# Second layer: where the hidden value of some routed and final items is kept, and which engine splits it

## The reference, cut to what matters

```
# second layer, L1
for e in range(2):                                  # shared experts
    h = silu(x @ s_w1[e].T) * (x @ s_w3[e].T);  shared += h @ s_w2[e].T
for e in range(8):                                  # routed experts, all computed, gates mostly zero
    h = gelu(x @ r_w1[e].T);                    routed += h @ r_w2[e].T * gates[:, e]
y = (shared / 2 + routed) / 4
out = x + (gelu((y @ U1) @ V1 + b1) @ U2) @ V2 + b2   # low-rank final block, 512 hidden features
```

## Time and profile before

| what | value |
|---|---|
| time, median of 3 runs | 890.18 us (889.91 to 892.35) |
| span of the profiled execution, first to last instruction | 886.9 us |
| what lies around the span, against the median | 3.3 us |
| TensorE busy | 870.3 us, 98% |
| VectorE busy | 682.8 us, 77% |
| ScalarE busy | 574.0 us, 65% |
| GpSimd busy | 402.0 us, 45% |
| granted TensorE clock | 1.000 of full |

### The profile page before, as it was taken

One profiled execution on the slowest core, in us unless ns is written; L12 is line 12 of the kernel. 1 busy time (PEld: TensorE's weight loads), 2 busy tenths in 40 slices (PEclk: granted clock), 3 DMA queues, 4 the chain that ended last, 5 costly groups with the idle time before them and its releaser, 6 DMA issues.

```text
span 886.9 us, 12606 instructions
## 1 busy us (share of the span) xinstructions
PE 870.3 (98%) x3838; PEld 690.2 (78%) x3838; DVE 682.8 (77%) x1094; ACT 574.0 (65%) x1029; POOL 402.0 (45%) x376
## 2 busy tenths in 40 slices
PE   8999999999999999999999999999999999999997
PEld 5788888777888888888888888888888777777773
DVE  7877777869689786686686686686665888998887
ACT  7888888765555455555555555555555678989895
POOL 7557783135356453253253252252232227754462
PEclk9999999999999999999999999999999999999999
DMA  9589981023113112012012012011010049582700
GB/s 311 211 276 313 293 295 35 1 86 135 48 48 111 42 42 84 4 45 84 1 48 83 1 48 84 0 48 48 1 48 0 1 108 209 106 178 53 161 25 36
DMA packets 36404, 83.23 MB, mean 94 GB/s; under 512 B 4464, under 2 KB 14320, under 8 KB 34544
## 3 DMA queue, kind: packets, MB, share of 16 engines
q1 hardware_dynamic: 36336, 82.42, 30.1%
HBM read 71.39 MB, written 6.83 MB: 88 GB/s over the span
## 4 chain that ended last, share of the span: by engine, by line
PE 76%; DVE 9%; issue 4%; ACT 3%; SPq 3%; DMA 2%; POOL 1%; DVEq 0%; ACTq 0%; POOLq 0%
PE ps L932 16%; PE ps L951 16%; PE ps L937 16%; PE ps L992 8%; PE ps L994 8%; PE ps L987 8%; DVE HL L1571 3%; SPq L658 1%; PE ps L974 1%; PE ps L972 1%; DVE Hf L1551 1%; DMA ST<-scratch 1%; DVE Hf L1558 1%; ACT HH L1084 1%; SPq L771 1%
## 5 line engine op out<-in xcount | busy, mean ns | idle before, releaser
L1078 ACT ACTIVATE Sg<-ps 128x512 f32<-128x512 f32 x288 | 171.7, 597 | 242.6 <-PE ps L951 242.3
L1551 DVE TENSOR_TENSOR Hf<-ps,Sg 128x512 f32<-128x512 f32 x288 | 197.9, 688 | 147.7 <-ACT Sg L1078 97.5
L1663 POOL TENSOR_TENSOR HL<-Hf,HH 128x512 fp32r<-128x512 f32 x130 | 174.2, 1347 | 157.4 <-ACT HH L1084 141.0
L1084 ACT ACTIVATE HH<-Hf 128x512 fp32r<-128x512 f32 x346 | 216.1, 625 | 21.1 <-DVE Hf L1551 14.4
L1571 DVE TENSOR_TENSOR HL<-Hf,HH 128x512 fp32r<-128x512 f32 x248 | 220.1, 888 | 4.3 <-ACT HH L1084 3.2
L932 PE MATMUL ps<-XHL,WBH 128*128 128x512 f32 x512 | 203.7, 398 | 1.8 <-DVE Hf L1551 1.8
L951 PE MATMUL ps<-XHL,WBH 128*128 128x512 f32 x512 | 202.2, 395 | 0.0
L937 PE MATMUL ps<-XHL,WBL 128*128 128x512 f32 x512 | 202.0, 395 | 0.0
L1678 POOL TENSOR_TENSOR XT<-XT,TMP 128x512 f32<-128x512 f32 x64 | 84.0, 1312 | 248.9 <-DVE TMP L1425 248.7
L932 PEld LDWEIGHTS ps<-XHL,WBH 128*128 128x128 f32 x512 | 96.0, 188 | 27.0 <-DVE Hf L1551 4.0
L951 PEld LDWEIGHTS ps<-XHL,WBH 128*128 128x128 f32 x512 | 96.0, 188 | 23.0
(11 more groups left out here) (275 smaller groups left out, 1327.6 us busy)
## 6 DMA issues: line engine op xcount, KB each, us to landing
CWB<-scratch SPq DMA_DIRECT2D x14, 1024.0 KB, 4.5
GWD<-expert_down SPq DMA_DIRECT2D x21, 576.5 KB, 4.4
GWU<-expert_up SPq DMA_DIRECT2D x21, 514.0 KB, 5.2
CWB<-scratch SPq DMA_DIRECT2D x40, 256.0 KB, 5.6
ST<-in_wb_dram SPq DMA_DIRECT2D x8, 768.0 KB, 6.2
ST<-scratch SPq DMA_DIRECT2D x24, 256.0 KB, 8.8
GX<-XT SPq DMA_DIRECT2D x68, 64.0 KB, 3.0
XT<-in_x_dram SPq DMA_DIRECT2D x8, 256.0 KB, 5.6
```

Of the source, the lines that this page charges most:

```text
L1078: e.activation(Sg[:, it.n % NG, :], zb[z % NZ][:, :], ACT.Silu).then_inc(s_act, 1)
L1084: e.activation(HH[:, it.n % NH, 0:it.cols], hidden_place(it), ACT.Copy).then_inc(s_hi_act, 1)
L1551: e.tensor_tensor(Hf[:, it.n % NS, :], zb[z % NZ][:, :], Sg[:, it.n % NG, :], ALU.mult).then_inc(s_prod, 1)
L1663: e.tensor_tensor(HL[:, it.n % NH, :], Hf[:, it.n % NS, :], HH[:, it.n % NH, :].bitcast(F32), ALU.subtract).then_inc(s_lo_pool, 1)
```

## The change

Routed items with ex % 4 == 3 and the even final items of blocks 0 to 4 become inplace: Gelu (F) or the gate multiply (R) writes the bank of z, and VectorE takes both parts from there. All other routed items and the odd early final ones have the high part on ScalarE and the low part on GpSimd. z_free gives the end of the low part for every in-place item, R included. The new function hf_free waits for the last item that did use the place in Hf, walking back over items in place. In the routed branch of VectorE the wait for Hf falls away for items in place.

```diff
--- before.py
+++ after.py
@@ -73,7 +73,7 @@
         self.cols = GROUPS[blk][1] * P if kind == "G" else BLK
 
         self.whole = kind == "F" and blk >= LATE and f % 2 == 1
-        self.inplace = kind in "AG"
+        self.inplace = kind in "AG" or (kind == "R" and ex % 4 == 3) or (kind == "F" and blk < LATE and f % 2 == 0)
 
 
 class Order:
@@ -356,10 +356,10 @@
                 lo[it.n] = s_down, it.n + 1
                 continue
             it.hi_act = it.kind in "BS" or (it.kind in "AG" and it.k % (8 if it.k < 16 else 4) != 0) or (
-                it.kind == "F" and it.blk < LATE and it.k % 2 == 1) or (it.kind == "R" and it.ex % 4 != 3)
+                it.kind == "R" and not it.inplace) or (it.kind == "F" and it.blk < LATE and not it.inplace)
             it.lo_pool = (it.kind == "B" and it.k % 4 == 1) or (
-                it.kind == "F" and ((it.blk, it.f) == (LATE + 1, 0) if it.blk >= LATE else it.k % 2 == 1)) or (
-                it.kind == "R" and it.ex % 4 != 1 and (it.blk, it.ex) != (NBLK - 1, 7)) or (it.kind == "S" and it.blk // 2 == 1)
+                it.kind == "F" and ((it.blk, it.f) == (LATE + 1, 0) if it.blk >= LATE else not it.inplace)) or (
+                it.kind == "R" and not it.inplace) or (it.kind == "S" and it.blk // 2 == 1)
             if it.hi_act:
                 n_hi_act += 1
                 hi[it.n] = s_hi_act, n_hi_act
@@ -383,11 +383,17 @@
 
         def z_free(z):
             it, j = z_users[z]
+            if it.inplace:
+                return lo[it.n]
             if it.kind == "R":
                 return s_gated, n_gated[it.n]
-            if it.inplace:
-                return lo[it.n]
             return (s_act, it.n + 1) if j == 0 else (s_prod, n_prod[it.n])
+
+        def hf_free(it):
+            n = it.n - NS
+            while real[n].kind in "RF" and real[n].inplace:
+                n -= NS
+            return lo[n]
 
         def sg_free(it):
             n = it.n - NG
@@ -1060,7 +1066,7 @@
                     e.wait_ge(s_z, z + 1)
                     if it.kind in "AGF":
                         if not it.inplace:
-                            e.wait_ge(*lo[it.n - NS])
+                            e.wait_ge(*hf_free(it))
                         if it.kind == "F":
                             bias = col("b1", it.f)
                         elif it.kind == "A":
@@ -1547,15 +1553,16 @@
                     z = it.z[1]
                     e.wait_ge(s_act, it.n + 1)
                     e.wait_ge(s_z, z + 1)
-                    e.wait_ge(*lo[it.n - NS])
+                    e.wait_ge(*hf_free(it))
                     e.tensor_tensor(Hf[:, it.n % NS, :], zb[z % NZ][:, :], Sg[:, it.n % NG, :], ALU.mult).then_inc(
                         s_prod, 1)
                 if k < len(items) and items[k] and items[k].kind == "R":
                     it = items[k]
                     e.wait_ge(s_act, it.n + 1)
                     e.wait_ge(f_gate[it.blk % 2][it.ex], 16 * (it.blk // 2 + 1))
-                    e.wait_ge(*lo[it.n - NS])
-                    e.tensor_tensor(Hf[:, it.n % NS, :], zb[it.z[0] % NZ][:, :], gate_place(it.blk, it.ex),
+                    if not it.inplace:
+                        e.wait_ge(*hf_free(it))
+                    e.tensor_tensor(hidden_place(it), zb[it.z[0] % NZ][:, :], gate_place(it.blk, it.ex),
                                     ALU.mult).then_inc(s_gated, 1)
                 if 1 <= k <= len(items) and items[k - 1] and not items[k - 1].whole:
                     it = items[k - 1]
```

## The result

| | before | after |
|---|---|---|
| time, median of 5 runs each | 890.35 us | 909.79 us |
| ratio after to before, 95% interval | | 1.0221 (1.0208 to 1.0234) |
| span of the profiled execution | 886.9 us | 908.0 us |
| TensorE busy | 870.3 us, 98% | 875.4 us, 96% |
| granted TensorE clock, mean | 1.000 | 0.994 |

The change makes the kernel 19.4 us slower. I had forecast 9.8 us slower, with a range that ended at 904. The sign and the three handovers as the main place were right, the size was not.

A forecast was written before the change was run, and what follows sets the result against it. TensorE, busy 98% of the span, was taken to bound the kernel. Terms 3.3 + 3.1 + 3.1 + 0.3 + 0.3 + 0.3 - 0.4 = 10.0 us put 890.2 at 900.2, stated as 900.0, range 893 to 904 us.

The forecast's parts named there:

- the three handovers: Routed to shared items, after 395, 427 and 459: the late bank costs 3.3, 3.1 and 3.1 us.
- The new wait and its three places: Sign: TensorE's up product waits for VectorE's HL three times, over 2.5 us each, near 745, 791 and 837 us.
- no more stretched splits in the routed stages: Sign: no VectorE split is stretched in routed and final stages, as PSUM sources avoid the stretch beside GpSimd.
- TensorE idle in block 2: Sign: TensorE is idle in the routed stretch of block 2, where it was not before.
- the relief: Final and routed stages: splits no longer stretched beside GpSimd gain 0.4 us, with ends 0 and 3.1 us.
- routed stretches: Routed items behind final ones 0.3 us, routed items without a backlog 0.3 us together.
- the end: After block 7, final items wait for ScalarE: 0.3 us under TensorE's lead, 1.7 us without it.
- part (3): What the change adds: z banks come free later, at handovers, routed items behind final ones and those without backlog.
- only takes away TensorE's lead on ScalarE: Routed items behind final ones, blocks 2, 4, 6: product 1.7 us late, mostly covered; 0.3 us, ends 0 and 5.1.
- one without a backlog: Routed items without a backlog: product of 387 0.1 us late, at some five places, 0.3 us together.
- the 4.47 of my sum: First handover, second up product of item 397: starts 4.47 us late, 3.1 us net of existing waits.
- my three: Kinds of place for late banks: routed to shared, routed behind final, routed without a backlog.

The follow-up runs named there:

- e_final: Kernel before with only the ten even final items in place, all routed items as before: 889.82 us against 889.18, ratio 1.0003.
- e_final_late: Kernel before with even final items in place except 404, 436 and 468, routed items as before: 890.25 us against 890.07, ratio 1.0000.
- e_first: Changed kernel, but VectorE splits a routed in-place item ahead of the next item's multiply instead of behind it: 896.07 us against 890.14, ratio 1.0063.
- e_hold16: Kernel before, but the z bank of all 16 routed items with ex 3 or 7 is freed only after their low part: 910.56 us against 890.14.
- e_clean: Changed kernel with the early split of e_first and items 395, 404, 427, 436, 459, 468, 487 kept in Hf: 895.18 us against 890.07, ratio 1.0058.
- e_sbuf: Changed kernel's engines for every high and low part, but no second-layer item in place (values in SBUF): 900.82 us against 889.18, ratio 1.0118.
- e_spread: e_sbuf with VectorE's low part of routed ex 3 and 7 one slot later, behind the next gate multiply: 900.14 us against 890.14, ratio 1.0121.
- e_sbuf_first: e_sbuf with the split of routed items with ex 3 or 7 ahead of the next multiply: 905.42 us against 890.07, ratio 1.0173.
- e_spare: Changed kernel, but items 395, 427, 459 and 487 go to Hf and are split on VectorE: 896.60 us against 889.18, ratio 1.0075.

## Why the prediction was wrong

**Right.** What bounds the kernel, and that nothing was to be won. The new wait and its three places: L938 on VectorE's HL, near 745, 791 and 837 us by my list, at 747, 798 and 847. Its size without the clock: 13.0 - 3.9 = 9.1 us against my 3.3 + 3.1 + 3.1 = 9.5; singly 3.5, 2.5 and 3.1, so the second was 0.6 smaller than I had it. The casts at 0.68 us, no more stretched splits in the routed stages (one cast of 1.03 us is left at 895.6, among the last final items), and TensorE idle in block 2. That the relief is worth next to nothing: e_final and e_final_late are level with before.

**The terms side by side.** Forecast for the span 10.0 us, measured 21.1. The 11.1 between them: routed stretches +6.0, clock +3.9, the end +1.0, the relief of 0.4 that didn't come, 0.4 ahead of item 380, handovers without the clock -0.4, final stretches -0.2.

**Wrong, the routed stretches: 0.6 us forecast, 6.6 measured** (about 1 of them the late DMA). This is the largest term, and the step that failed. In part (3) I wrote that a late bank behind final items "only takes away TensorE's lead on ScalarE", and that one without a backlog costs 0.1 us. Both were worked out from one item to the next, with everything else of before in its place. I never asked what stands behind the two passes in VectorE's queue. In block 2 of the changed kernel it is this:

```profile
782.05 0.68 DVE L1575 CAST HH<-ps 128x512 fp32r<-128x512 f32 x1
782.76 0.69 DVE L1578 TENSOR_TENSOR HL<-ps,HH 128x512 fp32r<-128x512 f32 x1
783.37 0.74 DVE L1542 SCALAR_TENSOR_TENSOR QS<-PH,sm,ps 128x512 fp32r<-128x512 f32 x1
784.03 0.68 DVE L1565 TENSOR_TENSOR Hf<-ps,CWB 128x512 f32<-128x512 f32 x1
```

```profile
782.84 0.60 ACT L1080 ACTIVATE ps<-ps 128x512 f32<-128x512 f32 x1
784.74 0.63 ACT L1090 ACTIVATE HH<-Hf 128x512 fp32r<-128x512 f32 x1 [1.31 <-DVE Hf L1565]
785.28 0.58 ACT L1080 ACTIVATE ps<-ps 128x512 f32<-128x512 f32 x1
```

The split of item 415, then an operation of the final block (QS), then the gates of 417. ScalarE waits 1.31 us for these gates with the Gelu of item 419, the next in-place item, behind it in its own queue. So 419 starts its chain late (Gelu 785.28 for a product of 783.51, 1.8 us instead of 0.9), its bank is free late, and the product of 423 waits in turn: a ring through three engines that closes every four items. TensorE waits at 419, 423 and 427 for 1.45, 0.74 and 0.33 us. The lead that I relied on wasn't being used up: from item 412 to 427 the products come 2.2 us later against before and ScalarE's Gelus 2.1, so ScalarE fell behind together with TensorE.

e_first shows the cure: with the split ahead of the multiply the same stretch loses 0.7 instead of 2.2 us. It moves the bank's release and the gates at once, so the ring itself is read from the trace and no run breaks it at one link. ScalarE's waits for gates alone aren't the cost: in e_first it still waits 10.4 us for them (13.3 in the changed kernel). Nor is the ring needed for a loss: in e_hold16 ScalarE waits only 1.3 us for gates, TensorE waits 2.0 us at item 419, and the Gelu of 427 starts 1.0 us behind its product instead of 2.4. There 1.4 us of lead were used up, as I had thought, and ScalarE was 1.5 us late besides.

**Wrong, the clock: not in the sum, about 3.9 us.** I priced a wait of TensorE at its length. Behind the first two handovers TensorE ran at 0.50 and 0.57 of its clock after having been idle for 4.5 and 2.9 us. Nothing in the trace of before shows a price for that, as its longest idle stretch in the second layer is 1.3 us; it belonged in the upper end of the range. The Trainium skill (TensorE: Matmul & The Clock Gate, section "What's actually happening") says that the clock granted follows how busy the engine has been, with half speed after idleness; the rows of the two waits agree. By that rule a forecast of three long waits should have had a second term; at the 1.6 to 2.3 us that one costs here, the range would have gone up by 5 to 7 us. The third wait of 2.95 us was followed by the full clock, so equal waits don't cost the same.

**Wrong, the first handover by its parts.** Its wait was 4.68 us gross, near the 4.47 of my sum, but both ends had moved by about as much (2.3 and 2.5 us), which was luck: before it, the product of 395 waited 1.2 us for the bank of 391, whose gates a DMA had brought late; the splits of 391 and the operation PS then stood ahead of the gates of 393.

**Small.** The end cost 1.3 us (2.7 less 1.4) instead of 0.3: the bank of item 468 holds item 472 for 2.0 us, and ScalarE's pace gives part of it back. This is a fourth kind of place that my three left out, the first even final item behind shared ones; item 440 waits as long for the bank of 436, but there all of it is made good by item 447.

**Open.** How much of the last 5 us of e_clean, and of e_sbuf's 10 to 12, is the new sharing itself: three low parts in a row on GpSimd and none between. In e_clean stretch can't be much of it, since from 722 us on only one subtraction (1.65 us) and one cast (1.13 us) of VectorE are stretched, and TensorE's own waits for held banks are 2.5 us; the rest isn't shown. For e_sbuf, e_spread rules out only that two passes share a slot, and e_sbuf_first changes order and stretch at once. A kernel with the new sharing and no bank held wasn't tried without stretch, since out of SBUF the stretch comes with it.

## What to carry to other kernels

A buffer that is handed back by the last step of a chain is as late as everything queued ahead of that step: before moving a release, walk the queue of the engine that will do it, and then ask what is queued behind it on the next engine, until the walk comes back to the first item. If it closes, the cost comes back with every turn (here 1.45, 0.74 and 0.33 us), because the engine on which the lead was counted falls behind too. If the release must stay there, put it ahead of the next item's work (here 13.5 us for one move), and price a long wait of TensorE with the slow products behind it.

## What the runs showed of the hardware that I had not expected

- TensorE's clock: fully busy from 752 to 757 us at 0.50 of the clock after 4.5 us idle, products 0.43 us apart; 0.57 after 2.9 us idle in one place, and 1.00 after 2.95 us idle in another of the same execution. In e_spare it fell twice after 1.84 us idle, and only five to six products after the wait; the same two waits of 1.84 us were followed by the full clock in the changed kernel.
- The same VectorE subtraction out of SBUF took 0.69 us undisturbed and 1.6 us on average in the sixteen places of e_sbuf_first, beside GpSimd; out of PSUM the longest was 0.694 us before, after and in e_first, though GpSimd was at work beside 24 of the 26 that the second layer has after.
